# Moving the value products of two cross-attentions directly behind the next unit's scores

## The reference, cut to what matters

```python
x = _layernorm(x + _L0_attn_ref(x, ...))                       # gated recurrence
x = _layernorm(x + _L0_xattn_ref(x, ctx, ctx, mask1, bias, ...))  # FIRST cross-attention
x = _layernorm(x + _L0_ffn_ref(x, ...))
x = _layernorm(x + _L1_attn_ref(x, ...))                       # self-attention
x = _layernorm(x + _L1_xattn_ref(ctx, ctx, x, mask2, ...))      # SECOND cross-attention
x = _layernorm(x + _L1_ffn_ref(x, ...))

# a cross-attention, for B=8, S=256, H=16, dh=16
q, k, v = (query @ Wq.T + bq), (key @ Wk.T + bk), (value @ Wv.T + bv)   # split into 16 heads
scores  = einsum('bhqd,bhkd->bhqk', q, k) / 4 (+ bias in the first) , masked
attn    = softmax(scores, axis=-1)
out     = einsum('bhqk,bhkd->bhqd', attn, v) -> (B, S, 256)
return out @ Wo.T + bo
```

## Time and profile before

| | us |
|---|---|
| device time, median of 3 runs | 966.96 (964.99 to 967.85) |
| the profiled execution, its own time | 966.73 |
| its span, first to last instruction | 964.8 |
| PE busy in the span | 869.2 (90%) |
| DVE busy | 684.7 (71%) |
| ACT busy | 612.9 (64%) |
| POOL busy | 409.4 (42%) |

### The profile page before, as it was taken

One profiled execution on the slowest core, in us unless ns is written; L12 is line 12 of the kernel. 1 busy time (PEld: TensorE's weight loads), 2 busy tenths in 40 slices (PEclk: granted clock), 3 DMA queues, 4 the chain that ended last, 5 costly groups with the idle time before them and its releaser, 6 DMA issues. The chain is left out here.

```text
span 964.8 us, 21262 instructions
## 1 busy us (share of the span) xinstructions
PE 869.2 (90%) x7001; PEld 621.0 (64%) x7001; DVE 684.7 (71%) x2527; ACT 612.9 (64%) x1596; POOL 409.4 (42%) x427
## 2 busy tenths in 40 slices
PE   7976999999999677999999999886899999999996
PEld 5755667767667545676777777664566666655564
DVE  5873888888896757577766666612788887876876
ACT  1322777777784347777777787822888888864441
POOL 0215326656642155255355352215435555336432
PEclk9997999999999899999999999997999999999999
DMA  8204410001003267976876877604000011000001
GB/s 305 85 0 142 138 35 4 23 23 34 2 12 135 84 184 237 284 243 207 270 226 206 262 251 230 189 15 146 5 26 26 26 29 31 17 2 1 23 23 45
DMA packets 96688, 101.87 MB, mean 106 GB/s; under 512 B 26862, under 2 KB 91886, under 8 KB 96327
## 3 DMA queue, kind: packets, MB, share of 16 engines
q1 hardware_dynamic: 96292, 100.46, 33.4%
q10 hardware_dynamic: 290, 0.09, 0.0%
HBM read 48.70 MB, written 51.82 MB: 104 GB/s over the span
## 5 line engine op out<-in xcount | busy, mean ns | idle before, releaser
L240 PE MATMUL bank<-x_feat,w_all_mats 128*128 128x256 f32 (+1 forms) x384 | 100.0, 407 | 12.3 <-DMA w_all_mats<-in_wmats 6.4
L240 PEld LDWEIGHTS bank<-x_feat,w_all_mats 128*128 128x128 f32 x384 | 73.6, 201 | 28.2 <-issue 9.6
L2660 POOL TENSOR_TENSOR bnd<-bnd,consts 128x60 f32<-128x60 f32 x64 | 18.1, 305 | 149.7 <-DMA bnd<-band_scratch 149.7
L2309 ACT ACTIVATE bias_area<-bias_area,mq_two 128x256 f32<-128x256 f32 x128 | 66.4, 532 | 0.0
L1344 PE MATMUL bank<-dist,rw 128*128 128x512 bf16 x288 | 64.3, 379 | 0.0
L779 ACT ACTIVATE q_heads<-bank 128x512 f32<-128x512 f32 x64 | 37.7, 590 | 39.8 <-PE bank L610 39.8
L1621 DVE COPY q_heads<-bank 128x512 f32<-128x512 f32 x64 | 42.7, 686 | 28.5 <-PE bank L1299 28.5
L2475 DVE COPY q_heads<-bank 128x512 f32<-128x512 f32 x64 | 41.3, 685 | 28.8 <-PE bank L2004 28.8
L858 DVE COPY q_heads<-bank 128x512 f32<-128x512 f32 x64 | 41.8, 684 | 25.7 <-PE bank L610 25.7
L771 ACT ACTIVATE Sx<-Sx,mq 128x256 f32<-128x256 f32 x128 | 54.4, 500 | 5.3 <-DVE mq L850 5.2
L1613 DVE CUSTOM_DVE_ANT_0 Sx<-bank,bias_area 128x256 f32<-128x256 f32 x128 | 46.5, 420 | 14.7 <-PE bank L1285 14.2
(11 more groups left out here) (271 smaller groups left out, 2459.9 us busy)
## 6 DMA issues: line engine op xcount, KB each, us to landing
dist<-skew_scratch SPq DMA_DIRECT2D x64, 296.0 KB, 4.1
skew_scratch<-rw SPq DMA_DIRECT2D x32, 588.0 KB, 4.6
bnd<-band_scratch SPq DMA_DIRECT2D x64, 108.0 KB, 2.8
band_scratch<-bias_area SPq DMA_DIRECT2D x32, 162.0 KB, 3.2
band_scratch<-bias_area SPq DMA_DIRECT2D x32, 148.0 KB, 2.3
w_all_mats<-in_wmats SPq DMA_DIRECT2D x16, 256.0 KB, 7.3
skew_scratch<-dist SPq DMA_DIRECT2D x4, 1024.0 KB, 8.7
context_values<-dist SPq DMA_DIRECT2D x8, 512.0 KB, 2.6
```

Source lines behind the costliest of these rows:

```text
L240: last = pe.matmul(dst[:, m * S:(m + 1) * S], w[:, k, m * P:(m + 1) * P], rhs[:, k, :], start=(k == 0), stop=(k == FT - 1))
L2309: last = act.activation(rows_of(n, g)[:, t, :], rows_of(n, g)[:, t, :], ACT.Exp, bias=mq_two[:, n % 2, g, t:t + 1], scale=-1.0, accum_out= ...
```

## The change

In both cross-attentions and in all four rounds `weigh(n - 1)` moves from the end of PE's round to directly behind `scores(n + 1)`, ahead of `turn(n, 2)`. On ACT the first exponentials `exps(n, 0)` move ahead of `turned(n - 1, 2)`, and `copy_ot(n - 2)` moves from the end of the round to behind `exps(n, 1)`, ahead of `copy_q` and `turned(n - 1, 3)`. DVE, POOL and SP are not touched, and no instruction is added or removed.

```diff
 def first_round(b, n):            # first cross-attention
     ...
     turn(n, 1)
     scores(n + 1)
+    if b >= 1:
+        weigh(n - 1)
     turn(n, 2)
     turn(n, 3)
     if b < B - 1:
         pe.wait_ge(v_sb, b + 1)
         project_k(b + 1)
-    if b >= 1:
-        weigh(n - 1)

 def second_round(b, n):
     ...
     scores(n + 1)
+    weigh(n - 1)
     turn(n, 2)
     turn(n, 3)
     ...
             turn_back(b - 1, 0)
-    weigh(n - 1)

 def third_round(b, n):
     ...
     scores(n + 1)
+    weigh(n - 1)
     if b >= 1:
         pe.wait_ge(normed, TT * b)
         transpose_tiles(pe, m_bank, at, at_mm)
     ...
             project_q(b + 2)
-    weigh(n - 1)
     if b >= 1:
         pe.wait_ge(at_sb, b)
     ...

 def fourth_round(b, n):
     ...
+    weigh(n - 1)
     turn(n, 2)
     turn(n, 3)
-    weigh(n - 1)

 # ACT, both cross-attentions
+            exps(n, 0)
             if n >= 1:
                 turned(n - 1, 2)
-            exps(n, 0)
             exps(n, 1)
+            if n >= 2:
+                copy_ot(n - 2)
             if j == 3 and b < B - 2:
                 copy_q(b + 2)
             if n >= 1:
                 turned(n - 1, 3)
             exps(n, 2)
             exps(n, 3)
-            if n >= 2:
-                copy_ot(n - 2)
             if j == 2 and b >= 1:
                 turn_at(b - 1)
```

## The result

The changed kernel takes 1018.99 us (median of 4 runs, 1014.72 to 1020.30) against 965.98 for the kernel before. The ratio is 1.054 with a 95% interval of 1.050 to 1.058: slower, as forecast, but 53 us instead of 40, and 2 us above the range.

The account below looks back on a forecast made before the run. Plain rounds were taken as bound by a ring of PE and ACT waits, neither engine full. 8.4 + 3.9 + 11.4 + 16.5 = 40.2, rounded to 40, gave 1006.5 us; range 988 to 1017.

Parts of the forecast that it names:

- Plain rounds: Ring of waits between PE and ACT grows from 5.14 to 5.62 us; 17 rounds, +8.4 us.
- PE's wait ahead of turn 1: Sign in a plain round of the second attention: about 1.1 us, released by the head-2 copy's pair.
- 0.5 ahead: Sign in a plain round: ACT's head-0 exponentials 0.5 us before the head-2 copy; S is the start of `scores(n+1)`.
- Fourth to first: First attention, fourth to first round: from 6.24 to 6.80 us, +0.56, seven times, +3.9 us.
- First to second: First attention, first to second round: PE keeps 6.0 us of work in either order, so 0.
- Third to fourth: Third round's scores to the next: 8.20 to 9.38 us, PE waiting for `copy_q`; whole class +16.5 us.
- Second to third: Second to third round: `normalise` waits for the later `turn_back`, 5.14 to 6.1 us; both attentions together +11.4 us.
- Rival 3: PE's clock falls to its lower level in one round per batch: +46 us, 1053 us; 3 in 100.
- Rivals 1 and 2: 1: only third rounds pay, 983 us, 12 in 100; 2: `weigh` hides in PE's waits, faster, 954, 5 in 100.

Follow-up runs that it names:

- experiment 2: Changed kernel's PE list with ACT's list of the kernel before: ratio 1.068 to the kernel before, 1027.7 us.
- ACT's list alone: Changed kernel's ACT list with PE's list of the kernel before: ratio 1.047 to the kernel before, 1007.5 us.
- experiment 1: Changed kernel, but in each batch's third unit (j = 2) `copy_ot(n-2)` stands behind `turned(n-1, 3)`: ratio 1.037 to the kernel before.
- experiment 8's first kernel: Kernel before, with ACT's copies `turned(n-1, 2)` and `turned(n-1, 3)` together ahead of `exps(n, 1)` in nearly all rounds: ratio 0.998 to the kernel before.
- experiment 5: Changed kernel plus eight unused identity matmuls behind the second `turn_back` in the first attention's third rounds: ratio 1.052 to the kernel before.

## Why the prediction was right in its direction and wrong in its size

- *Plain rounds, "New ring ... 5.62".* Right: 5.62 and 5.63. Its term for `weigh` was met by itself: +1.00 in experiment 2 (6.14). Its other two, -0.80 and +0.28, are the difference between 6.14 there and 5.62 here. PE's wait ahead of turn 1 came out at 0.93 where 1.1 was said. The sign "0.5 ahead" for the exponentials of head 0 doesn't follow from the prediction's own sum, which starts them at S + 1.7 and the copy at S + 2.77; the rows have 1.09.
- *Fourth to first.* Right in four of the seven, 6.78 against 6.80; batch 1 lost 0.47, batch 2 had a clock fall, and the last batch lost nothing (6.23).
- *First to second, "it keeps it in either order; 0".* Off by -0.3 each, 1.9 us in all: the same instructions of PE lie closer together, and their sum of 6.0 was too high. PE's list alone gives 6.14 there and ACT's list alone 6.70. No experiment was made on why both together give 5.70.
- *Third to fourth, "5.63 + 0.98 + 2.77 = 9.38".* Right: 9.36, `copy_q` at S + 5.61. Undoing it gives 8.20. Only the count was off, by the two stretches of batch 7.
- *Second to third, "Then 0.70 for normalise ... call it +0.9".* This is the step that failed. The sum followed DVE and came out near: 6.1, and 5.95 once nothing else is in the way (experiment 1). But the list of ACT has a second wait that I read past: `copy_ot(n-2)` at j = 2 overwrites a slot of `OTq` that the second `turn_back` still reads (L787, L1516). Before, `copy_ot` stood at the end of the list, where this wait was over. The move put it ahead of the copy that releases turn 1, with a wait of 1.07 us. I had checked for `weigh` which waits it brings along, and for `copy_ot` only its 0.28 us. This term was 21.6 instead of 11.4.
- *Rival 3, "PE's clock falls".* Given 3 in 100 and 46 us; it happened in part, 6.3 us in the profiled run. I priced it by all batches and set against it one wait that kept 1.00 in one profile; the same wait has a fall in that of experiment 8's first kernel. In the changed kernel the falls came in the first attention, mostly behind the stretch whose length I had underestimated. I had looked for them behind `project_q`, where no row shows one. The Trainium skill (TensorE: Matmul & The Clock Gate, Part 1: The HAM clock gate) says that the array slows down after it has been idle and speeds up after sustained work. The rows agree only in part: ahead of three of the falls PE was partly busy, for 2.2 of 4.20 us, and its longest single wait there was 1.11 us.
- Rivals 1 and 2 fall: plain rounds pay too, and PE doesn't leave its order.

With the wait of `copy_ot` in the sum it would have been 50, and the time 1017, at the edge of the range. What is left of the miss, 2.8 us, is the clock's 6.3 and the 1.1 outside these classes, less the 4.6 by which the other four classes came in below the forecast. That these nearly cancel is luck.

## What to carry to other kernels

When a step is moved, write down every semaphore it waits on, not only its duration: a wait that was over at the old place can be the last to end at the new one. Where a loop is bound by a ring of waits between engines, add up the ring before moving work: work that lies in both engines' idle time is free only outside it. And where stalls on PE get longer, look at the granted clock around the longest of them, stretch by stretch and in more than one profile, before calling it safe.

## What the runs showed of the hardware that I had not expected

- In batch 6 of the changed kernel PE's granted clock was 0.54 over the 3.67 us behind a 4.20 us stretch in which PE had been busy for 2.22 us; in experiment 5, with 3.09 us busy, it stayed at 1.00. It doesn't drop each time: it did behind three of the seven stretches from 2 to 3 (batches 1 to 7) of the first attention in one profile, and behind none of the second attention, where PE was busy for 2.75 us of the last 4.20. The stretch of 4.47 us with 2.26 us busy was followed by a fall in one kernel's profile and by none in another's.
- The second attention isn't free of falls. In experiment 2 three of its stretches from 1 to 2 ran at the lower level at their start, each behind a round with waits of PE of 1.04 and 0.71 us; other rounds with the same waits had none.
- Each of the four falls cost 1.5 to 1.7 us. The changed kernel's runs spread more, 1014.7 to 1020.3, with mean clocks of 0.973 and 0.965 at the two ends, against 964.1 to 967.9 before.
